# Score stacks of a four-block network in two sets and four row tiles of 32 partitions, with own shifts in the written order for the first and last sequences

## The reference

```
x = x + scan_block(norm(x))       # in-projection, causal conv of 4 taps, silu;  h = exp(delta*A)*h + B ;
                                  # 256 channels x 16 states; y = x_conv * (sum of h); gate; out-projection
x = x + expert_block(norm(x))     # gate by residual norms over 8 experts, top 2; sum of expert outputs
x = x + attention(norm(x))        # 16 heads
x = x + ffn(norm(x))              # 128 -> 512, two products, two 512 -> 512 layers with gelu, 512 -> 128
```

```
scores  = einsum('bhqd,bhkd->bhqk', Q, K)            # clipped at +-80, causal
weights = softmax(scores / sqrt(12))
attn    = einsum('bhqk,bhkd->bhqd', weights, V) @ W_O.T
```

## Time and profile before

| | |
|---|---|
| median of 3 runs | 1859.53 us (1855.02 to 1859.66) |
| the profiled execution | 1853.92 us |
| its span | 1849.2 us |
| its mean granted TensorE clock | 0.951 |
| TensorE busy | 1518.6 us (82%) |
| VectorE busy | 1541.3 us (83%) |
| ScalarE busy | 1286.7 us (70%) |
| GpSimd busy | 1112.0 us (60%) |
| DMA packets | 13773, 27.39 MB |

### The profile page before, as it was taken

The page is one execution under the profiler, slowest core; times in us unless marked ns, Lnnn a source line. Parts: engine busy times, 40 slices in busy tenths (PEclk is TensorE's granted clock), DMA queues, the critical chain, the costliest instruction groups (busy, mean ns, idle before and its releaser), DMA issues. The chain is left out here.

```text
span 1849.2 us, 24467 instructions
## 1 busy us (share of the span) xinstructions
PE 1518.6 (82%) x8039; PEld 807.2 (44%) x8039; DVE 1541.3 (83%) x2837; ACT 1286.7 (70%) x2176; POOL 1112.0 (60%) x987
## 2 busy tenths in 40 slices
PE   4246888888888888888888888888886699999997
PEld 2022333333433333343333334333332478888886
DVE  5899999999999999999999998996330488988883
ACT  5666898888888888888888888884543444444441
POOL 4885775858677585866758686674111255555552
PEclk9566999999999999999999999999998799999998
DMA  4000110101001010100101010010400000000000
GB/s 131 0 1 4 15 17 1 18 1 18 7 12 18 1 18 1 18 8 11 18 1 18 1 18 11 8 18 1 82 7 11 0 1 12 12 12 13 17 12 19
DMA packets 13773, 27.39 MB, mean 15 GB/s; under 512 B 3069, under 2 KB 3782, under 8 KB 13130
## 3 DMA queue, kind: packets, MB, share of 16 engines
q1 hardware_dynamic: 13642, 25.78, 7.2%
HBM read 9.00 MB, written 4.19 MB: 7 GB/s over the span
## 5 line engine op out<-in xcount | busy, mean ns | idle before, releaser
L584 POOL TENSOR_TENSOR sum_fast<-sum_fast,state_fast 128x512 f32<-128x512 f32 x448 | 574.0, 1281 | 122.1 <-DVE state_fast L566 84.1
L566 DVE TENSOR_TENSOR_SCAN state_fast<-state_fast,bank 128x512 f32<-128x512 f32 x512 | 602.1, 1201 | 1.6 <-ACT bank L535 1.6
L967 ACT ACTIVATE prob_fast<-bank 128x1024 f32<-128x1024 f32 x320 | 326.4, 1020 | 173.7 <-PE bank L951 172.1
L951 PE MATMUL bank<-stacks_fast 64*128 64x512 f32 (+3 forms) x2048 | 367.1, 467 | 71.3 <-ACT prob_fast L967 58.3
L551 ACT ACTIVATE state_fast<-chan_all_kept,neg_a_fast 128x512 f32<-128x512 f32 x512 | 342.8, 713 | 13.6 <-POOL sum_fast L584 12.4
L1011 POOL TENSOR_SCALAR_AFFINE_SELECT prob_fast<-prob_fast 128x512 f32<-128x512 f32 x256 | 166.4, 662 | 294.7 <-ACT prob_fast L967 293.8
L951 PEld LDWEIGHTS bank<-stacks_fast 64*128 64x128 f32 x2048 | 172.1, 187 | 282.0 <-ACT prob_fast L967 157.1
L1028 PE MATMUL bank<-prob_fast,v_ext_fast 128*32 128x512 f32 (+3 forms) x2048 | 175.9, 444 | 14.5 <-POOL prob_fast L1011 14.2
L638 PE MATMUL bank<-resid_m_fast,xnt_g_fast 128*128 128x512 f32 x256 | 145.2, 656 | 45.8 <-DVE gate_fast L719 32.0
L669 PE MATMUL bank<-we_t_fast,xnt_g_fast 128*128 128x512 f32 x256 | 141.3, 645 | 2.6 <-DVE own_fast L790 2.6
L1390 PE MATMUL bank<-cell_a_fast,w_all_fast 128*128 128x512 f32 x512 | 131.2, 398 | 0.3 <-POOL cell_a_fast L1586 0.3
(11 more groups left out here) (204 smaller groups left out, 2618.6 us busy)
## 6 DMA issues: line engine op xcount, KB each, us to landing
stacks_fast<-parts_fast SPq DMA_DIRECT2D x64, 128.0 KB
stacks_fast<-rest_fast SPq DMA_DIRECT2D x64, 64.0 KB
out_x<-f_out_fast SPq DMA_DIRECT2D x16, 256.0 KB, 2.0
x_res_kept<-in_x SPq DMA_DIRECT2D x1, 2048.0 KB, 14.7
chan_all_kept<-in_h_t SPq DMA_DIRECT2D x2, 1024.0 KB, 15.8
x_res_kept<-in_x SPq DMA_DIRECT2D x1, 1024.0 KB, 10.4
chan_all_kept<-in_w_t SPq DMA_DIRECT2D x3, 256.0 KB, 12.7
x_res_kept<-in_x SPq DMA_DIRECT2D x2, 256.0 KB, 2.9
```

Source lines behind the costliest of these rows:

```text
L566: dve.tensor_tensor_scan(h[:], h[:], self.banks[0][:], 0.0, ALU.mult, ALU.add).then_inc(self.v_scan.sem)
L584: pool.tensor_tensor(total[:], total[:], h[:], ALU.add).then_inc(self.p_sum.sem)
L951: ins = pe.matmul(self.scores[:, c:c + SEQ - P * kt], rows[:, 1, h // 2, P * kt:P * kt + P], rows[:, 0, h // 2, P * kt:SEQ], start=True, s ...
L967: act.activation(self.probs[u % 2][:, i * 1024:(i + 1) * 1024], self.scores[:], ACT.Exp, scale=SCALE).then_inc(self.a_prob.sem)
```

## The change

The one set of stacks becomes two sets [128, 2, 4, 512] of half the size, taken in turn by sequences of even and odd number. A head now has a block of 32 partitions, of which 12 hold numbers. Head h lies in row tile `h % 2 + 2 * (h // 4 % 2)`, at column `h // 8 * 2 + h // 2 % 2`. A score step still works on two heads in two row tiles: 0 and 32 for groups 0 and 2, 64 and 96 for groups 1 and 3. The DMAs of a sequence wait for the scores of the sequence two before. There are 16 in place of 8, each with half the bytes, and counts that depend on them are adapted. The columns of the projection weights are laid out anew to match.

All planned times of phase one are new, and a table `EDGES` gives the parts of sequences 0, 13, 14 and 15 a shift of their own, where there is one. Parts keep their content; which of them changes its place is set by the numbers.

```diff
@@ sp_rows
-        sp, parts, stacks, rot = self.sp, self.parts, self.stacks, self.rest[0]
+        sp, parts, stacks, rot = self.sp, self.parts, self.stacks[b % 2], self.rest[0]
         yield
         sp.wait_ge(self.p_t_rot.sem, self.p_t_rot.at(b))
-        if b:
-            sp.wait_ge(self.t_score.sem, self.t_score.at(b - 1, 5 * GROUPS - 1))
+        if b > 1:
+            sp.wait_ge(self.t_score.sem, self.t_score.at(b - 2, 5 * GROUPS - 1))
         else:
-            sp.wait_ge(self.p_stacks.sem, self.p_stacks.at())
-        for r in (0, 64):
-            sp.dma_start(stacks[r + DH:r + DQK, 0], rot[r // 2:r // 2 + NQ // 2]).then_inc(self.stack_r.sem, 16)
+            sp.wait_ge(self.p_stacks.sem, self.p_stacks.at(0, b))
+        for h in range(4):
+            r, n = 32 * h, NQ // 4
+            sp.dma_start(stacks[r + DH:r + DQK, 0], rot[n * h:n * h + n]).then_inc(self.stack_r.sem, 16)
             sp.dma_start(stacks[r + DH:r + DQK, 1], rot[NQ:ROPE_ROWS].unsqueeze(1).to_broadcast(
-                [DR, PAIRS, SEQ])).then_inc(self.stack_r.sem, 16)
+                [DR, QUADS, SEQ])).then_inc(self.stack_r.sem, 16)
         for i in range(2):
             yield
             sp.wait_ge(self.a_t_qk.sem, self.a_t_qk.at(b, i))
-            for r in (0, 64):
-                sp.dma_start(stacks[r:r + DH, i], parts[r:r + 64, i]).then_inc((self.stack_q, self.stack_k)[i].sem, 16)
+            for h in range(4):
+                r = 32 * h
+                sp.dma_start(stacks[r:r + DH, i], parts[r:r + 32, i]).then_inc((self.stack_q, self.stack_k)[i].sem, 16)
@@ pe_scores
-                    rows = stacks[64 * (h % 2):64 * (h % 2) + 64]
-                    ins = pe.matmul(self.scores[:, c:c + SEQ - P * kt], rows[:, 1, h // 2, P * kt:P * kt + P],
-                                    rows[:, 0, h // 2, P * kt:SEQ], start=True, stop=True, tile_position=(64 * (h % 2), 0))
+                    r, c4 = 32 * (h % 2 + 2 * (h // 4 % 2)), h // 8 * 2 + h // 2 % 2
+                    rows = stacks[r:r + 32]
+                    ins = pe.matmul(self.scores[:, c:c + SEQ - P * kt], rows[:, 1, c4, P * kt:P * kt + P],
+                                    rows[:, 0, c4, P * kt:SEQ], start=True, stop=True, tile_position=(r, 0))
@@ order
+EDGE_OF = {0: 0, NSEQ - 3: 1, NSEQ - 2: 2, NSEQ - 1: 3}
+
+def place(period, name, b, k, edges):
+    shift = EDGES[name][EDGE_OF[b]] if edges and name in EDGES and b in EDGE_OF else 0
+    return period * b + TIMES[name][k] + shift
+
@@ TIMES and EDGES: the strands that the prediction speaks of
-PERIOD, F_PERIOD = 78826, 24000
+PERIOD, F_PERIOD = 78828, 24000
-    "sp_rows": [236612, 244449, 262646],
+    "sp_rows": [250242, 270940, 284246],
-    "pe_s_out": [105457],
+    "pe_s_out": [105227],
-    "pe_scores": [203061, 206712, 210127, 211906, 212752, 218421, 220191, 221756, 225635, 230028, 233012, 236030,
-        238938, 243841, 244836, 246508, 250105, 253149, 258508, 260547],
+    "pe_scores": [203281, 206618, 210865, 212035, 212491, 218346, 220269, 222085, 224925, 230290, 232485, 236009,
+        238202, 244799, 245955, 246608, 249503, 254428, 255951, 261032],
-    "pe_bound": [265919],
+    "pe_bound": [247717],
-    "dve_setup": [-65717, -48779, -18943, -17968, -16808, -12885],
+    "dve_setup": [-75226, -28484, -10656, -10248, -9514, -9465],
-    "dve_s_head": [-20017, -12889, -7920, 12843, 17928, 21459],
+    "dve_s_head": [-19202, -14854, -7636, 11834, 17464, 21370],
-    "pe_values": [210177, 216686, 219526, 221752, 223371, 231041, 234330, 237530, 242565, 246311, 247251, 251115,
-        258893, 263255, 264524, 267412],
+    "pe_values": [211877, 213343, 218671, 220344, 223391, 230905, 234568, 236628, 242740, 246486, 247841, 250879,
+        258844, 262697, 264535, 266987],
-    "pe_t_out": [270351, 271838],
+    "pe_t_out": [271672, 273819],
-    "act_scores": [202759, 207082, 211090, 212302, 214034, 217813, 222387, 223555, 227340, 230817, 234204, 238260,
-        240384, 242483, 245583, 249636, 251803, 255073, 257206, 258841],
+    "act_scores": [203089, 207145, 211030, 211850, 214190, 217366, 222690, 223153, 227581, 230659, 234209, 238332,
+        240291, 243386, 245757, 248537, 251870, 254860, 257376, 260167],
-    "act_t_rstd": [171027],
+    "act_t_rstd": [169803],
...
+EDGES = {
...
+    "act_scores": [0, 0, 0, 12087],
...
+    "act_t_rstd": [1601, 1738, -270, -1773],
...
+    "dve_s_head": [3537, 0, 0, -1],
...
+    "pe_scores": [0, 0, 0, -910], "pe_t_out": [-630, 1451, 8263, 5500], "pe_t_proj": [-1414, 0, 0, -88],
+    "pe_t_turn": [-1766, 1660, -1034, 924], "pe_values": [0, 0, 0, -282], "pool_masks": [210, 0, -833, -18771],
...
+    "sp_rows": [0, 0, 22633, 1609],
+}
```

More of the change, by code:

```diff
@@ L80 @@
+    "pool_t_proj": [181817],
+    "pool_masks": [208544, 210594, 215832, 223564, 231498, 234826, 236890, 243933, 247375, 256568, 259694, 261669],
     "sp_f": [128010],
@@ new lines @@
+    "act_g_rstd": [109502],
+    "act_g_turned": [113480],
+    "act_g_squares": [116086, 118689, 120013, 121502, 124212, 126452, 130033, 132877],
+    "act_g_gate": [134955, 136242, 145506, 148300],
+    "act_s_rstd": [-115246],
+    "act_s_turned": [-34149],
+    "act_s_xn": [-108123],
+    "act_g_xn": [109831],
+    "act_t_xn": [172431],
+    "dve_g_norm": [108034],
+    "dve_g_sums": [119407, 121556, 124170, 126491, 127717, 129303, 132558, 133575],
+    "dve_g_gate": [134938, 135860, 140401],
@@ new lines @@
+    "dve_g_experts": [151157, 153930, 155001, 157075, 157444, 159651, 161398, 162074, 163318],
+    "pe_t_turn": [173144],
+    "pe_t_proj": [177081, 177583, 183382, 186937, 187790, 188602],
+    "act_t_rstd": [169803],
+    "act_t_turned": [173261],
+    "act_t_proj": [185332, 186611, 187602],
+    "dve_t_norm": [166278],
+    "dve_t_proj": [175798, 178699, 188105, 189932],
+    "pe_g_setup": [-13071, 5678, 9877, 32806, 35255, 74227],
+    "act_g_setup": [5398, 20818, 45114, 62100, 104514],
+    "pe_t_setup": [-3961, 10452, 88017],
@@ L194, with in_order @@
 DONE = object()
-def in_order(period, strands):
-    parts = [[period * b + TIMES[name][0], rank, 0] for rank, (name, b, _) in enumerate(strands)]
+EDGE_OF = {0: 0, NSEQ - 3: 1, NSEQ - 2: 2, NSEQ - 1: 3}
+def place(period, name, b, k, edges):
+    shift = EDGES[name][EDGE_OF[b]] if edges and name in EDGES and b in EDGE_OF else 0
+    return period * b + TIMES[name][k] + shift
+def in_order(period, strands, edges=False):
+    parts = [[place(period, name, b, 0, edges), rank, 0] for rank, (name, b, _) in enumerate(strands)]
     for _, _, strand in strands:
@@ L209, in in_order @@
         else:
-            part[0], part[2] = period * b + TIMES[name][k + 1], k + 1
+            part[0], part[2] = place(period, name, b, k + 1, edges), k + 1
 class Program:
@@ L303, in phase_one_room @@
         self.v_ext = [sb(f"v_ext{i}", [P, NT, HEADS * VW + 32 - VW]) for i in range(2)]
-        self.stacks = sb("stacks", [P, 2, PAIRS, SEQ])
+        self.stacks = [sb(f"stacks{i}", [P, 2, QUADS, SEQ]) for i in range(2)]
         self.probs = [sb(f"prob{i}", [P, GROUP * SEQ]) for i in range(2)]
@@ L856, in act_t_proj @@
                 moved = (self.stack_q, self.stack_k)[i]
-                act.wait_ge(moved.sem, moved.at(b - 1, 1))
+                act.wait_ge(moved.sem, moved.at(b - 1, 3))
                 if i == 0 and not general:
@@ L938, in pe_scores @@
     def pe_scores(self, b):
-        pe, stacks = self.pe, self.stacks
+        pe, stacks = self.pe, self.stacks[b % 2]
         for g in range(GROUPS):
@@ L1197, in pool_setup @@
         pool.memset(self.eps[:], EPS).then_inc(self.p_eps.sem)
-        pool.memset(self.stacks[:], 0.0).then_inc(self.p_stacks.sem)
+        for stacks in self.stacks:
+            pool.memset(stacks[:], 0.0).then_inc(self.p_stacks.sem)
         for v in self.v_ext:
@@ L1216, in sync_program @@
             strands.append(("sp_rows", b, self.sp_rows(b)))
-        in_order(PERIOD, strands)
+        in_order(PERIOD, strands, not general)
     def tensor_program(self, general):
```

129 lines of the change are left out of this document (60 added, 69 removed).

## The result

The changed kernel took 1974.86 us (median of 4 runs, 1969.89 to 1983.58) against 1859.28 (4 runs, 1855.02 to 1859.66): a ratio of 1.0632, 95% interval 1.0592 to 1.0673. The forecast was 1860, within 1846 to 1882, and it had no change as the likeliest case. The profiled execution took 1974.45 us with a span of 1970.7; it stands for the median.

What follows compares the result with a forecast made beforehand. VectorE was taken to set the steady pace; DMAs +0.8, order +0.6, head +0.3 and tail +0.5 made +2.2 us, giving 1856.1 on the profiled execution, 1861.7 on the median; forecast 1860 between them, range 1846 to 1882.

Steps and rivals of the forecast that it cites:

- Changed: score matmuls read 32 instead of 64 rows: Score steps in phase one: work goes by columns, narrower tiles drop only zero rows, so 0 us.
- rival 2: Narrower score tiles cost TensorE, by more half clock or less overlap: +16 to +34 us, 1876 to 1894; chance 0.10.
- The signs of being wrong: Period moving over 0.3 us, score steps over 1.3 us at full clock, or stages after 1324.8 changing by over 5 us.
- The third sign: Score steps on TensorE lasting over 1.3 us at full clock, where 1.13 us was expected, would show the forecast wrong.
- Overlap of tiles 0 and 32: Score steps: if these tiles did not overlap as 0 and 64 do, +1.1 us per exposed step, upper bound 19.
- The removed wait: DMAs no longer wait for the previous sequence's scores; L901 releases them 0.95 us later anyway, so gain 0.
- Twice as many DMAs: Stack transfers, 16 half-sized for 8: landing 0.4 us later, hidden thirteen times, exposed in the last two sequences, +0.8 us.
- Rival 1: Small DMAs land too late, past the 1.4 us slack before scores: 3 us later gives +27, 1886; chance 0.15.
- The order in steady state: Phase one's neighbour swaps: only values.13 ahead of s_out.0 touches VectorE's path, 0.05 us per period, +0.6 us in all.
- the three gaps: VectorE's waits per period: 1.8 us on L669's expert banks, 0.9 on L1035's transposes, 0.5 on ScalarE's L488.
- the swap that I priced: On TensorE, values.13 goes ahead of s_out.0, delaying VectorE's L606: 0.05 us per period, bounds 0 to 1.
- Own shifts: Moved parts at the head (sequence 0), net +0.3 us, and at the tail (13 to 15), net +0.5 us.

Runs made afterwards that it cites:

- Low tiles only: The kernel before, each score matmul reading the first 32 rows of its head's 64; one set of stacks, 8 DMAs, old order: 2077.87 us, ratio 1.114.
- High tiles: The changed kernel with 64-row score tiles at 0 or 64, each matmul summing the products of two heads: 1867.04 us, ratio 1.0037.

## Why the prediction was wrong

The step that failed is "Changed: score matmuls read 32 instead of 64 rows", put at 0, and with it the size of rival 2. Two pairs of kernels show it. Low tiles only differs from the kernel before in the height alone: +219 us. High tiles (1867) and the changed kernel (1975) have the same sets, DMAs and order and differ in the height, with it in the tiles' places and so the rows that are read: -108 us, nearly all of the loss of 116. What the runs showed in place of the 0 is a granted clock that falls to half for 47.8 us of every 174.1.

- *Mechanism.* Rival 2 named it, "its clock is granted at half more often when only 64 of 128 rows work", with a chance of 0.10 and a price of 17 x 0.95 + 1.4 per period = +34. Measured: +18 in the last sequence's steps, where I had said 16, but 6.5 per period in place of 1.4, a size that I had worked out from no row. I had priced half clock by the score steps, as if only they slowed. TensorE was busy for 85% of the steady stretch, so at half clock it needs more time than there is, and every wait on it grows.
- *The argument against it.* "The clock was full for 805 us, in which score steps are a small share of what TensorE does" was a wrong reading. They were 367.1 of TensorE's 1518.6 us over the whole execution, a quarter, and they come together. A clock at 1.00 says nothing of how far from falling it is; the tail, where it did fall, was the hint.
- *The signs of being wrong.* The period moved by 6.5 us, where 0.3 was to be the sign, and the stages from the first score step of sequence 14 on grew by 32.6, where 5 was. The third sign, a score step over 1.3 us at full clock, did not come: a step's length at full clock cannot show a fall of the clock.
- *Overlap of tiles 0 and 32.* Right: 1.13 us a step, and the upper bound of 19 us did not arise. The Trainium skill, "TensorE: Matmul & The Clock Gate", "Why this matters for your kernels", has a single matmul of 32 rows take as long as one of 128. The trace agrees: 1.13 us for a step of 32 rows, for one of 64, and for L638's two matmuls of 128 rows. But the cost of low tiles is in the clock, not in the matmul.
- *The removed wait.* Right: L901's line (L932 after) releases the first DMA of all 16 sequences, and the first score step still comes 19.55 us behind it (19.53 before).
- *Twice as many DMAs.* Right that it is hidden, and nothing in the tail either: in the last sequence 17.3 us from the first issue (1482.34) to the first score step (1499.67), for 17.5. I took 0.4 twice. Rival 1 fell: the transfers cost 3.3 us more to issue (11.2 in all, just over the 8 to 11 I had said) and landed no later. That is also against what the rules for kernel authors of the Trainium skill's "DMA: Bandwidth & Descriptors" would make of transfers under 64 KB.
- *The order in steady state.* Right in sign, wrong in size and place: 0.48 us per period, not 0.05, and from a swap that I had passed over with "none of the swaps reaches the places of the three gaps". It reached the first by way of TensorE's values.3. That swap makes 0.44 of the 0.48; the 0.04 left bound all the others, and do not speak against the 0.05 of the swap that I priced. That undoing it left the period at 81.04 says less, since the wait behind values.0 still stood.
- *Own shifts.* Summed at +0.8; 5.9 by the experiments, with wide error, and by the profiled executions most of it in the tail, which I had at +0.5. Which of the shifts do it is open.

## What to carry to other kernels

Before lowering the rows of a matmul on a busy TensorE, ask what the granted clock would do, not only what the matmul takes: the same columns in the same time cost 6% here, and 11% in low tiles only, because all of TensorE's work slowed. Price a fall of the clock by all the work that TensorE has in that stretch against its idle time. And follow a moved part through the engine that waits for it: 0.68 us in front of a short VectorE part lengthened the period by 0.44.

## What the runs showed of the hardware that I had not expected

TensorE's granted clock falls with lower row tiles at unchanged columns and unchanged lengths of a step at full clock: steady clock 1.00 with tiles of 64 rows, 0.94 with half the steps at 32, 0.87 and 0.77 with all. Rows that hold zeros count as rows. The height of a tile, the rows at work at once (64 for 128) and the rows of the weight loads changed together in every kernel here, so which of the three counts is not shown. The loss is not in proportion to the low steps (50 us for half, 219 for all), and the same height has two patterns, of about 1975 and about 2070 us, into which even one program can fall.
